# Tail fill, edge-list load and router width in a graph network kernel

## The chip, the cores and the metric

The program runs on one core of one Trainium2 chip. The metric is the device time of one execution in microseconds. Engines: TensorE (PE; its weight loads are shown as PEld), VectorE (DVE), ScalarE (ACT), GpSimd (POOL) and SyncE (SP). SP, ACT and POOL issue DMAs, each on a queue of its own.

## The reference, cut to what matters

Two layers over 6,250 nodes of 256 features and 100,000 edges sorted by destination. Layer 0: a graph step (sum of `x[src]` by `dst`, two products with batch norm between) beside linear attention over all nodes, then a mixture of 32 experts in which each node goes to one. Layer 1: two weighted graph convolutions beside a second attention, then slice attention.

```python
x = x + gnn0(xn, src, dst, edge_weight, ...) + attention0(xn)
# the mixture that the change touches, xf = layernorm(x)
logits = xf @ router_w.T + router_b          # 32 columns
idx = argmax(logits, axis=-1)
h   = relu(einsum('nd,ndh->nh', xf, W1[idx]) + b1[idx])   # 256 -> 64
out = relu(einsum('nh,nhd->nd', h, W2[idx]) + b2[idx])    # 64 -> 256
x = x + out
x = x + gcn1(layernorm(x), src, dst, edge_weight) + attention1(layernorm(x))
x = x + slice_attention(layernorm(x))
```

## The kernel before, in words

The kernel is a row of stages. Inside a stage each engine has its own program, and semaphores order them. A stage ends in a barrier of all engines, after which POOL clears the stage's semaphores and a second barrier follows, so time saved inside one stage moves all that follows forward. Most stages walk over 25 units of up to 256 nodes (49 tiles of 128) through `pipeline`, which interleaves an engine's steps at fixed lags in program order.

1. `stage_setup` (lines 231 to 403). POOL fills constants; SP loads the edge lists (lines 259 to 262: `src`, `dst`, `edge_weight`, each as 97 rows of 1,024 edges and one row of 672), waits for all six loads, then loads 18 weights and bias vectors (line 254) and writes `d_dst` (line 281). DVE waits for the six loads at line 335, casts and checks, and PE and DVE then turn the four lists in 32 rounds over two PSUM banks: one transpose of 98 x 128 (line 389), one copy of 128 x 98 (line 353). Then the weights are turned (lines 399 and 403).
2. `stage_front` (line 406): layer norm, keys and values of the first attention.
3. `stage_aggregate` three times (one for layer 0, two for layer 1): POOL gathers 784 tiles of 128 source rows by indirect DMA (line 1222), DVE builds a selection matrix, PE multiplies (line 1293). Not touched.
4. `stage_gnn_first` and `stage_gnn_second`: batch norm and products.
5. `stage_route` (lines 1736 to 1945). Per unit: ACT ReLU (1812), PE turns back (1908), DVE adds (1841) and takes moments, POOL the root (216), DVE normalises into `accT` (222), PE turns (118), ACT copies to `xnT` (1818), PE multiplies by the router `rT` of 32 columns (1921), DVE adds the bias (1847) and picks the expert; per two units PE counts ranks (1933 to 1937), DVE makes the slots (1871 to 1876), and POOL scatters four tiles of rows into `d_xs` (1803), where each expert owns a region of 50 pages of 128 rows. After the last unit DVE writes `tail_row`, the first free row of each region (1880), and the tables of which expert and page each of 80 tiles has (1881 to 1899).
6. `stage_experts` (line 1948). 80 tiles. For tile t POOL reads the page number from `tile_page` and loads 128 rows (`xt`, 1997), SP loads two weights of the tile's expert (2010, 2011), PE turns the tile (2023), DVE copies (2056), PE multiplies (2032), ACT ReLU (2084), PE multiplies (2040), ACT ReLU (2090) and ACT sends `y` (2094). Buffers are four deep. Behind the last row of each region 128 rows have to be zero. These fills, one DMA of 128 x 256 zeros per expert (1982), are made here: ACT fills the even experts, POOL the odd ones, one ahead. Before POOL loads tile t < 32 it waits for the fill of expert t. ACT issues the fill of expert t+2 after it has seen that of t landed, and in its program order after the `send` of tile t-2; POOL issues the fill of t+2 ahead of the load of t. After tile 31 there are no fills.
7. `stage_second_front`, the second and third aggregation, `stage_heads`, `stage_out`.

The wait that ties loads to fills, and the order in which ACT takes its steps:

```python
if t % 2 == 1 and t + 2 < EXPERTS:
    fill(pool, t + 2, filled_pool)
if t < EXPERTS:
    pool.wait_ge((filled_pool if t % 2 else filled_act)[t // 2 % 2], 16 * (t // 4 + 1))
...
tiles(act, (refill, 0), (relu_h, 0), (relu_y, 1), (send, 1))
```

Of the kernel before, what the change touches and what calls it, by code (L numbers as in the profile page):

```python
# [230 lines left out]
def stage_setup(nc, kit, a, d):  # L231

    k = kit
    with Stage(nc, kit) as st:
# [13 lines left out]
        nload = [0]  # L248

        with nc.Block() as block:  # L250
            @block.sync
            def _(sp):
                def load(dst, src):
                    sp.dma_start(dst, src, allow_slow_non_contiguous=True).then_inc(wld, 16)
                    nload[0] += 1
                full, rest = E // GE, E % GE
                sp.wait_ge(mset, 1)
                for n, name in enumerate(("src", "dst")):
                    sp.dma_start(epad_i[0:full, n, :], a[name][0:full * GE].rearrange("(g e) -> g e", e=GE)).then_inc(eld, 16)
                    sp.dma_start(epad_i[full:full + 1, n, 0:rest], a[name][full * GE:E].rearrange("(g e) -> g e", g=1)).then_inc(eld, 16)  # L260
                sp.dma_start(eew[0:full, :], a["edge_weight"][0:full * GE].rearrange("(g e) -> g e", e=GE)).then_inc(eld, 16)
                sp.dma_start(eew[full:full + 1, 0:rest], a["edge_weight"][full * GE:E].rearrange("(g e) -> g e", g=1)).then_inc(eld, 16)
                sp.wait_ge(eld, 96)
# [17 lines left out]
                sp.dma_start(d.dst.rearrange("(g e) -> g e", e=GE), epad_i[0:NG, 1, :]).then_inc(eld, 16)  # L281
                sp.wait_ge(eld, 112)
                sp.wait_ge(wld, 16 * nload[0])
# [40 lines left out]
            def _(dve):  # L324
# [9 lines left out]
                dve.wait_ge(eld, 96)  # L334
# [15 lines left out]
                for out, _ in dst:  # L350
                    for u in range(GT):
                        dve.wait_ge(tdone, kk + 1)
                        dve.tensor_copy(out.rearrange("p (g u) -> p g u", u=GT)[:, :, u], k.bank[kk % 2][:, 0:NG]).then_inc(cdone, 1)
                        kk += 1
# [20 lines left out]
            def _(pe):  # L375
# [10 lines left out]
                for x in (esrc, edst, rel, eew):  # L386
                    for u in range(GT):
                        b = go()
                        pe.transpose(b[:, 0:NG], x[0:NG, u * P:(u + 1) * P], k.ident[0:NG, 0:NG]).then_inc(tdone, 1)
# [1345 lines left out]

def stage_route(nc, kit, a, d):
# [4 lines left out]
    with Stage(nc, kit) as st:  # L1741
# [4 lines left out]
        tstart = st.sb("tstart", [P, EXPERTS])  # L1746
        with Stage(nc, kit) as sr:
# [10 lines left out]
            count = sr.sb("count", [P, EXPERTS])  # L1758
            ones = sr.sb("ones_h", [P, P], BF16)
# [8 lines left out]
            r_done, back, x1_done, turned, xnT_done, lg_psum, lg_done, ranked, one_done, placed, counted, slot_done, numbered, tab_done, tab_turned = (  # L1768
                sr.sem(n) for n in "r_done back x1_done turned xnT_done lg_psum lg_done ranked one_done placed counted slot_done numbered tab_done tab_turned".split())
            gpool = sr.sem("gpool")  # L1770
            sent = sr.pool_dma("sent")
# [9 lines left out]
            with nc.Block() as block:  # L1781
                @block.sync
                def _(sp):
# [7 lines left out]
                    pipeline(sp, (load, 0), (store, 3))  # L1791
                    x1.all_sent(sp)

                @block.gpsimd
                def _(pool):
# [8 lines left out]
                    pipeline(pool, (lambda u: nm.root(pool, u, gpool), 2), (scatter, 7))  # L1804
                    pool.wait_ge(sent, 16 * NTILE)

                @block.scalar
                def _(act):
# [10 lines left out]
                    pipeline(act, (relu, 0), (copy_xnT, 3))  # L1819

                @block.vector
                def _(dve):
                    n = [0]

                    def then(ins):
                        n[0] += 1
                        ins.then_inc(ranked, 1)
                        dve.wait_ge(ranked, n[0])
                    dve.memset(one[:, LASTT:NTILE, :], 0.0)
# [726 lines left out]
```

## Time and profile before

| what | value |
|---|---|
| runs shown | 4180.55, 4184.23, 4201.93 us (median 4184.23) |
| profiled execution | 4179.45 us, span 4178.0 us |
| busy share | PE 70%, PEld 53%, DVE 44%, ACT 19%, POOL 63% |
| mean granted TensorE clock | 0.858 |
| DMA | 501.67 MB, mean 120 GB/s |

The stages lie at these times of the span, read off their first and last rows: setup 0 to 77.4 us, front to 196.4, first aggregation to 1240, batch-norm stages to 1373.5, routing to 1520.2, experts to 1767, second front to 1898, the other aggregations to 3985, heads and output to 4178.

A page's busy share is a mean over all of these. For a change that touches three stages, the views cut to those stages are the ones to read. In a timeline row the columns are start, duration, engine, line, operation, tiles and count; in brackets is the idle time before it and what ended it. A timeline row with a count above 1 merges neighbours, and its duration is from the first start to the last end. One product in 32-bit floats is two records of PE; a transpose is one.

### The profile page before, as it was taken

What the parts mean: (1) busy time and instruction counts of PE and PEld (TensorE: products, weight loads), DVE (VectorE), ACT (ScalarE), POOL (GpSimd) and SP (SyncE); (2) the same over time, 40 slices, a digit from 0 to 9 for tenths busy, and PEclk for the clock granted to TensorE, in tenths of its full rate; (3) what the DMA queues carried; (4) which work ended last, traced back from release to release, by engine and by line L of the source; (5) the groups of instructions that cost most, each with busy time, mean ns of one, the idle gap of its engine ahead of it and who ended that gap; (6) DMA issues with size and microseconds to landing.
All of it is one profiled execution on the core that took longest, in us unless ns stands there. A gap on an engine that the chain in (4) does not pass through costs nothing. (4 is left out here: it accounts for less than half of the span.)

```text
span 4178.0 us, 41741 instructions
## 1 busy us (share of the span) xinstructions
PE 2928.2 (70%) x13016; PEld 2216.1 (53%) x13016; DVE 1827.8 (44%) x3387; ACT 781.5 (19%) x1777; POOL 2616.7 (63%) x2695
## 2 busy tenths in 40 slices
PE   2867777777768745696776766666577777777768
PEld 2755555555544633584655544444355555555547
DVE  3644444444444730273333333332255555555533
ACT  0411111111113311231111111000022222222220
POOL 1277777777760331256777777777577777777701
PEclk9988888888888556998888888888699999999969
DMA  1334444444432433683444433333344444444405
GB/s 61 99 115 119 120 120 119 120 119 119 118 104 90 138 104 115 193 278 105 119 119 116 120 106 110 106 109 110 92 121 126 126 126 126 127 127 125 124 26 187
DMA packets 280442, 501.67 MB, mean 120 GB/s; under 512 B 61259, under 2 KB 180689, under 8 KB 280074
## 3 DMA queue, kind: packets, MB, share of 16 engines
q0 software_dynamic: 126528, 346.64, 28.9%
q1 hardware_dynamic: 139852, 139.57, 10.7%
q10 hardware_dynamic: 13824, 12.59, 0.9%
q8 instruction: 113, 1.85, 0.2%
q14 instruction: 125, 1.02, 0.1%
HBM read 412.72 MB, written 85.58 MB: 119 GB/s over the span
## 5 line engine op out<-in xcount | busy, mean ns | idle before, releaser
L1293 PE MATMUL bank<-g,m 128*128 128x256 f32 (+1 forms) x4704 | 1568.4, 461 | 923.9 <-DMA g<-d_t,src_i 590.7
L1222 POOL DMA_INDIRECT g<-d_t,src_i x1568 | 1572.5, 1003 | 521.1 <-issue 520.8
L1293 PEld LDWEIGHTS bank<-g,m 128*128 128x128 f32 x4704 | 924.2, 224 | 1253.1 <-issue 574.3
L1222 POOL DMA_INDIRECT g<-d_xn,src_i x784 | 791.9, 1010 | 255.1 <-issue 255.1
L1244 DVE TENSOR_TENSOR eq<-iota,rel_f 128x1024 bf16<-128x1024 f32 x294 | 357.7, 1217 | 457.4 <-PE bank L1293 400.7
L1257 DVE TENSOR_TENSOR accT<-bank,accT 128x256 f32 x294 | 122.7, 417 | 573.2 <-PE bank L1281 572.9
L1247 DVE TENSOR_TENSOR m<-eq,ew_f 128x1024 f32<-128x1024 bf16 x294 | 360.1, 1225 | 10.1
L1228 ACT ACTIVATE s<-bank 128x256 f32<-128x256 f32 (+1 forms) x294 | 111.6, 380 | 1005.6 <-PE bank L1293 551.8
L1997 POOL DMA_DIRECT2D xt<-d_xs x80 | 43.0, 538 | 168.9 <-issue 166.7
L1163 PE MATMUL bank<-wg,side_lg 128*128 128x256 f32 (+1 forms) x392 | 142.7, 457 | 2.9 <-DVE side_lg L1155 2.9
L1295 PE MATMUL bank<-ones_b,eq 128*128 128x1 bf16 x784 | 139.6, 178 | 0.0
L216 POOL TENSOR_TENSOR rsd<-ved,mhalf 128x2 f32<-128x2 f32 (+1 forms) x25 | 18.8, 754 | 188.5 <-DVE ved L210 188.3
L171 POOL DMA_DIRECT2D out<-y x25 | 17.8, 714 | 177.4 <-DVE y L2406 177.4
L2056 DVE COPY xT<-bank 128x256 f32<-128x256 f32 x80 | 34.0, 425 | 200.0 <-PE bank L2023 200.0
L1281 PE MATMUL bank<-ident,s 128*128 128x128 f32 x588 | 119.9, 288 | 0.0
L1255 DVE TENSOR_TENSOR dinv<-bank,dinv 2x128 f32 x98 | 27.4, 279 | 188.8 <-PE bank L1281 188.8
L2023 PE MATMUL bank<-ident,xt 128*128 128x128 f32 x160 | 41.6, 350 | 92.4 <-DMA xt<-d_xs 92.2
L216 POOL TENSOR_TENSOR rsa<-vea,mhalf 128x2 f32<-128x2 f32 (+1 forms) x25 | 17.5, 701 | 141.0 <-DVE vea L210 141.0
L1295 PEld LDWEIGHTS bank<-ones_b,eq 128*128 128x128 bf16 x784 | 87.5, 112 | 34.5
L676 DVE SCALAR_TENSOR_TENSOR side_q<-side_e,side_q 128x256 f32<-128x256 f32 (+1 forms) x49 | 20.9, 427 | 182.7 <-ACT side_q L669 182.7
L1128 PE MATMUL bank<-wxs,m 128*128 128x512 f32 (+1 forms) x196 | 95.6, 611 | 2.7 <-ACT m L1120 2.7
L1281 PEld LDWEIGHTS bank<-ident,s 128*128 128x128 f32 x588 | 84.8, 150 | 23.5 <-issue 3.7
(386 smaller groups left out, 4401.5 us busy)
## 6 DMA issues: line engine op xcount, KB each, us to landing
g<-d_t,src_i POOLq DMA_INDIRECT x1568, 2.8
g<-d_xn,src_i POOLq DMA_INDIRECT x784, 2.8
side_xn<-d_xn SPq DMA_DIRECT2D x96, 128.0 KB, 2.5
d_x<-x SPq DMA_DIRECT2D x48, 256.0 KB, 3.6
d_swT<-wkv SPq DMA_DIRECT2D x48, 256.0 KB, 3.7
swT<-d_swT SPq DMA_DIRECT2D x24, 512.0 KB, 3.4
xt<-d_xs POOLq DMA_DIRECT2D x80, 128.0 KB, 2.6
d_ys<-y ACTq DMA_DIRECT2D x80, 128.0 KB, 2.3
```

The costliest lines, as they stand in the source:

```text
L1128: ins = pe.matmul(k.bank[6][0:w, :], self.xnT3[i % 2][:, c, 0:w], k.wxs[:, c, :], start=(c == 0), stop=(c == C - 1))
L1163: pe.matmul(k.bank[3 + q // 2][:, q % 2 * D:(q % 2 + 1) * D], sw, self.xn3[i % self.LG][0:w, :], start=(i == 0 and q % 2 == 0), stop=last ...
L1222: pool.indirect_dma_start(g[n % RING][:, u, 0:D], None, table, bass.IndirectOffsetOnAxis(ap=k.src_i[:, t:t + 1], axis=0)).then_inc(gathere ...
L1228: act.activation(s[n % 2][:], k.bank[n % 2][:, 0:SW], ACT.Copy).then_inc(copied, 1)
L1244: dve.tensor_tensor(eq[r][:], k.iota[:].rearrange("p (a n) -> p a n", a=1).to_broadcast([P, GT, P]), k.rel_f[:, e].rearrange("p (u a) -> p ...
L1247: dve.tensor_tensor(m[r][:], eq[r][:], k.ew_f[:, e].rearrange("p (u a) -> p u a", a=1).to_broadcast([P, GT, P]), ALU.mult).then_inc(m_done, 1)
L1257: dve.tensor_tensor(at, chunks(k.bank[7]), at, ALU.add).then_inc(acc_added, 1)
L1281: ins = pe.transpose(k.bank[7][:, c * P:(c + 1) * P], s[n % 2][:, c * P:(c + 1) * P], k.ident[:])
L1293: ins = pe.matmul(b[:, 0:GW], m[o][:, u, :], g[r][:, u, :], start=(u == 0), stop=(u == GT - 1 and not count))
L1295: ins = pe.matmul(b[:, GW:SW], eq[o][:, u, :], k.ones_b[:, 0:1], start=False, stop=(u == GT - 1))
L1997: pool.dma_start(xt[r][:], pages[bass.ds(x, 1), :, :].rearrange("a p d -> p (a d)")).then_inc(x_loaded[r], 16)
L2023: ins = pe.transpose(k.bank[j][:, c * P:(c + 1) * P], xt[r][:, c::C], k.ident[:])
```

## The change

- Setup: each list is loaded as 96 rows of 1,024, one row of 1,024 cut into 16 parts, and one row of 672 cut into 16 parts: nine DMAs on SP. The weights are loaded by ACT, which waits for nothing. Four transposes go into one bank, and one copy of 392 columns takes them out: 8 rounds in place of 32.
- Routing: the router is copied into `wide_rT`, whose columns 32 to 127 are zero, so each router product has 128 columns; the bias add reads the first 32.
- Tails: the `zero` tile and the fills move into the routing stage. When `tail_row` is written, SP fills experts 0, 3, ..., 30 (11 fills), ACT 1, 4, ..., 31 (11) and POOL 2, 5, ..., 29 (10, behind its scatters). Semaphores count runs of four fills of one queue, and POOL waits for a tile's run ahead of its load.

```diff
@@ stage_setup
+                for to, name in ((epad_i[:, 0, :], "src"), (epad_i[:, 1, :], "dst"), (eew[:], "edge_weight")):
+                    for g, n, w in ((0, even, GE), (even, full - even, GE), (full, 1, rest)):
+                        sp.dma_start(to[g:g + n, 0:w].rearrange("g (c e) -> g c e", c=(16 if n == 1 else 1)),
+                                     a[name][g * GE:g * GE + n * w].rearrange("(g c e) -> g c e", g=n, c=(16 if n == 1 else 1))).then_inc(eld, 16)
+                sp.wait_ge(eld, EDGE_LOADS)
+                sp.dma_start(d.dst.rearrange("(g e) -> g e", e=GE), epad_i[0:NG, 1, :]).then_inc(eld, 16)
+            @block.scalar
+            def _(act):
                 def load(dst, src):
-                    sp.dma_start(dst, src, allow_slow_non_contiguous=True).then_inc(wld, 16)
+                    act.dma_start(dst, src, allow_slow_non_contiguous=True).then_inc(wld, 16)
...
-                    for u in range(GT):
+                    for u in range(0, GT, 4):
                         b = go()
-                        pe.transpose(b[:, 0:NG], x[0:NG, u * P:(u + 1) * P], k.ident[0:NG, 0:NG]).then_inc(tdone, 1)
+                        for q in range(4):
+                            ins = pe.transpose(b[:, q * NG:(q + 1) * NG], x[0:NG, (u + q) * P:(u + q + 1) * P], k.ident[0:NG, 0:NG])
+                        ins.then_inc(tdone, 1)
@@ new class
+class Tails:
+    QUEUES, RUN = 3, 4
...
+    def fill(self, eng, q):
+        for n, e in enumerate(range(q, EXPERTS, self.QUEUES)):
+            row = eng.value_load(self.k.tail_row[0:1, e:e + 1], min_val=0, max_val=EXPERTS * REGION * P - P)
+            eng.dma_start(self.d.xs[bass.ds(row, P), :], self.zero[:]).then_inc(self.filled[q][n // self.RUN], 16)
+    def landed(self, eng, e):
+        if e < EXPERTS:
+            q, n = e % self.QUEUES, e // self.QUEUES
+            run = n // self.RUN
+            total = len(range(q, EXPERTS, self.QUEUES))
+            eng.wait_ge(self.filled[q][run], 16 * min(self.RUN, total - run * self.RUN))
@@ stage_route
+                    sp.wait_ge(tails_known, 1)
+                    tails.fill(sp, 0)
                     x1.all_sent(sp)
...
                     pipeline(pool, (lambda u: nm.root(pool, u, gpool), 2), (scatter, 7))
+                    pool.wait_ge(tails_known, 1)
+                    tails.fill(pool, 2)
                     pool.wait_ge(sent, 16 * NTILE)
...
-  ins = pe.matmul(k.bank[2 + u.n % 2][0:w, j * EXPERTS:(j + 1) * EXPERTS], xnT[u][:, c, j * P:j * P + w], k.rT[:, c, :], ...)
+  ins = pe.matmul(k.bank[2 + u.n % 2][0:w, j * P:(j + 1) * P], xnT[u][:, c, j * P:j * P + w], wide_rT[:, c, :], ...)
@@ stage_experts
-                    if t % 2 == 1 and t + 2 < EXPERTS:
-                        fill(pool, t + 2, filled_pool)
-                    if t < EXPERTS:
-                        pool.wait_ge((filled_pool if t % 2 else filled_act)[t // 2 % 2], 16 * (t // 4 + 1))
+                    tails.landed(pool, t)
...
-                tiles(act, (refill, 0), (relu_h, 0), (relu_y, 1), (send, 1))
+                tiles(act, (relu_h, 0), (relu_y, 1), (send, 1))
```

## Rows read from the trace of the kernel before

**Rows 1.** Groups of the page: gathers of layer 1 (busy, mean ns, idle before).

```profile
L1222 POOL DMA_INDIRECT g<-d_t,src_i x1568 | 1572.5, 1003 | 521.1 <-issue 520.8
```

**Rows 2.** Waits in the setup (total us, times, longest).

```profile
DVE esrc L335 <- DMA eew<-in_edge_weight: 38.5, 1, 38.5
```

**Rows 3.** Windows of the setup: span; busy by engine; PEclk, DMA share, GB/s.

```profile
23.00:52.00 29.00, 0.00 (x0) 0.00 (x0) 0.00 (x0) 0.00 (x0) 0.00 (x0) 1.00 0.06 26
52.00:62.00 10.00, 2.85 (x10) 1.74 (x10) 7.62 (x20) 0.00 (x0) 0.00 (x0) 1.00 0.64 190
```

**Rows 4.** Timeline of the setup, in order of time.

```profile
3.84 0.35 SPq L259 DMA_DIRECT2D epad_i<-in_src  x1
...
7.79 5.70 DVE L333 CAST iota<-iota_i 128x128 f32<-128x128 int32 x1 [7.79 <-POOL mhalf L318]
7.97 5.44 POOL L320 MEMSET dinv<- 128x6400 f32 x1
...
58.08 0.56 PE L389 MATMUL bank<-ident,esrc 98*128 98x98 f32 x2 [58.08 <-DVE okc L347]
...
71.34 0.56 DVE L353 COPY ew_f<-bank 128x98 f32<-128x98 f32 x2 [0.29 <-PE bank L389]
```

**Rows 5.** Single lines: copies out of PSUM in the setup, ns min/median/max.

```profile
L353 DVE COPY ew_f<-bank x8: 332/334/338, 68.8 to 71.6; 128x98 f32<-128x98 f32 x8
L367 DVE COPY w2T<-bank x2: 424/424/425, 74.8 to 75.3; 128x256 f32<-128x256 f32 x2
```

**Rows 6.** Windows of routing, of tiles 0 to 29 and of tiles 30 to 79.

```profile
1374.00:1499.00 125.00, 94.73 (x492) 85.81 (x492) 98.12 (x361) 38.97 (x75) 59.23 (x67) 0.50 0.46 145
1520.20:1664.70 144.50, 68.22 (x233) 53.64 (x233) 14.66 (x41) 18.00 (x57) 26.04 (x48) 0.59 0.37 113
1664.70:1764.00 99.30, 78.94 (x408) 57.89 (x408) 24.66 (x53) 32.55 (x103) 25.78 (x48) 0.96 0.68 197
```

**Rows 7.** Timeline: four router products; two products of 128 columns.

```profile
1424.67 1.91 PE L1921 MATMUL bank<-rT,xnT 128*128 128x32 f32 x8
...
1529.64 1.06 PE L2032 MATMUL bank<-xT,w 128*128 128x128 f32 x4
```

**Rows 8.** Groups of lines in routing: the router product (busy, mean ns, idle before).

```profile
L1921 PE MATMUL bank<-rT,xnT 128*128 128x32 f32 (+1 forms) x196 | 46.8, 403 | 2.1 <-ACT xnT L1818 2.1
```

**Rows 9.** Waits in routing.

```profile
DVE lgall L1847 <- PE bank L1921: 15.4, 13, 3.2
```

**Rows 10.** The end of routing: timeline, and POOL's drain at the barrier (ns).

```profile
1500.72 0.17 DVE L1880 SCALAR_TENSOR_TENSOR tail_row<-iota,count 1x32 int32<-1x32 f32 x1
...
1507.69 1.57 POOL L1803 DMA_INDIRECT d_xs<-accT,slot  x1 [0.30 <-issue]
...
1520.19 0.27 DVE L2045 MEMSET zero<- 128x256 f32 x1 [15.41 <-PEq L92]
L1781 POOLq DRAIN  x1: 4048/4048/4048, 1513.7 to 1513.7; - x1
```

**Rows 11.** Timeline of the experts: tile 0, tile 30, tile 79.

```profile
1521.85 0.63 POOL L1982 DMA_DIRECT2D d_xs<-zero  x1 [12.59 <-issue]
1524.42 0.57 POOL L1997 DMA_DIRECT2D xt<-d_xs  x1 [1.93 <-issue]
1525.60 0.55 POOL L1982 DMA_DIRECT2D d_xs<-zero  x1 [0.62 <-issue]
1526.95 0.68 PE L2023 MATMUL bank<-ident,xt 128*128 128x128 f32 x2 [22.85 <-DMA xt<-d_xs]
...
1664.70 0.70 PE L2023 MATMUL bank<-ident,xt 128*128 128x128 f32 x2 [5.42 <-DMA xt<-d_xs]
...
1758.76 0.40 PE L2023 MATMUL bank<-ident,xt 128*128 128x128 f32 x2
```

**Rows 12.** Waits in the experts' first 144 us.

```profile
PE bank L2023 <- DMA xt<-d_xs: 92.2, 20, 22.8
```

More of the change, by code:

```diff
@@ L248, in stage_setup @@
         nload = [0]
+        EDGE_LOADS = 16 * 9
         with nc.Block() as block:
@@ L1733, in own_rows, with __init__ @@
     return Kept(lambda u: k.accT[:, :, u.n * BODY:(u.n + 1) * BODY])
+class Tails:
+    QUEUES, RUN = 3, 4
+    def __init__(self, st, k, d, zero):
+        self.k, self.d, self.zero = k, d, zero
+        runs = -(-EXPERTS // (self.QUEUES * self.RUN))
+        self.filled = [[(st.pool_dma if q == 2 else st.sem)(f"filled{q}_{r}") for r in range(runs)] for q in range(self.QUEUES)]
+    def fill(self, eng, q):
[8 more added lines that the diff above has]
+            eng.wait_ge(self.filled[q][run], 16 * min(self.RUN, total - run * self.RUN))
 def stage_route(nc, kit, a, d):
@@ L1767, in stage_route @@
             nm = PipedNorm(sr, "d", x1, xn=own_rows(k))
-            r_done, back, x1_done, turned, xnT_done, lg_psum, lg_done, ranked, one_done, placed, counted, slot_done, numbered, tab_done, tab_turned = (
-                sr.sem(n) for n in "r_done back x1_done turned xnT_done lg_psum lg_done ranked one_done placed counted slot_done numbered tab_done tab_turned".split())
+            r_done, back, x1_done, turned, xnT_done, lg_psum, lg_done, ranked, one_done, placed, counted, slot_done, numbered, tab_done, tab_turned, widened = (
+                sr.sem(n) for n in "r_done back x1_done turned xnT_done lg_psum lg_done ranked one_done placed counted slot_done numbered tab_done tab_turned widened".split())
             gpool = sr.sem("gpool")
+            tails_known = sr.sem("tails_known")
             sent = sr.pool_dma("sent")
@@ L1819, in _ @@
                     pipeline(act, (relu, 0), (copy_xnT, 3))
+                    act.wait_ge(tails_known, 1)
+                    tails.fill(act, 1)
                 @block.vector
@@ L1828, in then @@
                         dve.wait_ge(ranked, n[0])
+                    dve.memset(wide_rT[:, :, EXPERTS:P], 0.0).then_inc(widened, 1)
+                    dve.tensor_copy(wide_rT[:, :, 0:EXPERTS], k.rT[:]).then_inc(widened, 1)
+                    then(dve.memset(zero[:], 0.0))
                     dve.memset(one[:, LASTT:NTILE, :], 0.0)
@@ L1879, in _ @@
                     dve.wait_ge(counted, BATCHES)
-                    dve.scalar_tensor_tensor(out=k.tail_row[:], in0=k.iota[0:1, 0:EXPERTS], scalar=float(REGION * P), in1=count[0:1, :], op0=ALU.mult, op1=ALU.add)
+                    dve.scalar_tensor_tensor(out=k.tail_row[:], in0=k.iota[0:1, 0:EXPERTS], scalar=float(REGION * P), in1=count[0:1, :], op0=ALU.mult, op1=ALU.add).then_inc(tails_known, 1)
                     then(dve.tensor_scalar(pages_i[:], count[:], float(P - 1), None, ALU.add))
@@ L1967, in stage_experts @@
         sent = [st.sem(f"y_sent{j}") for j in range(DEEP)]
[L1968 to L1969 removed]
+        mine_done, start_done = st.sem("mine_done"), st.sem("start_done")
         padded, turned, xT_done, hid, h_done, out_psum, y_done = (st.sem(n) for n in "padded turned xT_done hid h_done out_psum y_done".split())
@@ L1978, in tiles @@
                         step(p - lag)
-        def fill(eng, e, done):
-            r = eng.value_load(k.tail_row[0:1, e:e + 1], min_val=0, max_val=EXPERTS * REGION * P - P)
-            eng.dma_start(d.xs[bass.ds(r, P), :], zero[:]).then_inc(done[e // 2 % 2], 16)
         with nc.Block() as block:
@@ L2044, in _ @@
             def _(dve):
-                dve.memset(zero[:], 0.0).then_inc(blank, 1)
                 for j in range(DEEP):
@@ L2071, in _ @@
             def _(act):
-                act.wait_ge(blank, 1)
-                fill(act, 0, filled_act)
-                def refill(t):
-                    if t % 2 == 0 and t + 2 < EXPERTS:
-                        act.wait_ge(filled_act[t // 2 % 2], 16 * (t // 4 + 1))
-                        fill(act, t + 2, filled_act)
                 def relu_h(t):
```

39 lines of the change are left out of this document (16 added, 23 removed).

## The prediction

> **What bounds the kernel now.** The page's busy shares are read first and put aside: PE is at 70%, POOL at 63%, and no engine is full. Three quarters of the span are three aggregations paced by POOL's gathers, 1,568 in layer 1 [rows 1] and half as many in layer 0, and the change touches none of them. What it touches lies in three stages separated by barriers, so each stage's own last wait is the one to read.
>
> Setup: waits, then windows, then the timeline. DVE waits 38.5 us for the last edge list [rows 2]. In that time DMA moves 26 GB/s at a share of 0.06, which is one engine of 16 (1/16 = 0.0625); the loads after it move 190 GB/s at 0.64 [rows 3]. Then 32 rounds of turn and copy run from 58.08 to 71.34 + 0.56 = 71.90 [rows 4].
>
> Experts: the first PE row of a tile shows its place. Tiles 30 to 79 come at a pitch of (1758.76 - 1664.70)/49 = 1.92 us; tiles 0 to 30 take 1664.70 - 1526.95 = 137.75 us, 4.59 us each [rows 11]. In the slow part PE waits 92.2 us for `xt` [rows 12] and is half idle (68.2 busy in 144.5 us; 78.9 in 99.3 in the other part [rows 6]). The difference in code is the fill: `xt` waits for a fill, and ACT issues the next one only after earlier tiles have gone through.
>
> Routing: DVE is the busiest with 98.1 of 125 us, and PE has 94.7 at half clock, 1.2 GHz [rows 6]. DVE waits 15.4 us in all for the router product [rows 9].
>
> **The change, part by part.**
>
> *Edge lists.* What is late once the lists come fast is DVE itself: its cast of `iota` takes 5.70 us beside POOL's memset of `dinv` and ends at 7.79 + 5.70 = 13.49 [rows 4]. The lists are 1.2 MB and held one engine for 1.2/0.026, about 46 us, so 46/16 = 2.9 us of all 16. The weights and `d_dst` take 0.64 x 10 = 6.4 us of all 16 [rows 3]. Were both queued at 3.84 [rows 4], all would be moved by 3.84 + 9.3 = 13.1 and, with some 2 us to land, known at 15. But ACT starts its weights earlier, since it waits for nothing, and only the lists matter to DVE: at best nine issues at about 0.5 us end at 8.3, and the lists land by 11. I take 13.49, with 0 to +2 us; there is no gain beyond, as the cast is untouched. DVE starts on the lists at 13.49 where it started at 52.0 (13.49 + 38.5): **-38.5 us**. The weights are wanted only after the rounds.
>
> The trace shows no load of 96 rows. The Trainium skill, "DMA: Bandwidth & Descriptors", section "Why a DMA increments its semaphore by 16 and not by 1", says that a transfer is split over the largest number of engines up to 16 that divides the slowest dimension of both sides. That makes 97 rows one engine, as the row of 26 GB/s shows, and 96 rows sixteen. By that rule the term is -38.5; were it wrong for this shape, the term would be 0, which is rival D.
>
> *Rounds.* A turn is one record of 128 columns. Four such records take 1.06 us at half clock [rows 7], of which the last one's 0.40 [rows 8] is latency, so (1.06 - 0.40)/3 = 0.22 us from start to start, 0.88 a round of four. The copy of 392 columns is not shown: it lies between 0.42, the copy of 256, and 4 x 0.334 = 1.34 [rows 5]. From 98 to 256 columns the slope is 0.57 ns, which would give 0.50, but this copy writes with a stride; I take 0.65, nearest the longer copy's row. With two banks PE sets the round: 8 x 0.88, plus 0.2 for the last turn's latency and 0.65 for the last copy, 7.9 us. Before: 71.90 - 58.08 = 13.8. **-5.9 us**; with copies of 1.34 it is 8 x 1.34 + 1 = 11.7, so -2; with turns of 98 columns cheaper in proportion, -7.
>
> *Router.* Four products (8 records) of 32 columns take 1.91 us, two of 128 columns (4 records) 1.06, both at half clock [rows 7]. Start to start that is (1.91 - 0.40)/7 = 0.216 and (1.06 - 0.40)/3 = 0.22: the narrow record already comes as slowly as the wide one, so padding costs PE's stream nothing, and at most 0.05 us a unit at the end, 1 us. The copy and two memsets at the stage's head (0.6 us of DVE) lie in DVE's wait for the first rows; uncovered they cost that. I take **0**; the bounds are +2 and -12 (rival B).
>
> *Fills, at the end of routing.* SP and ACT have nothing left but waits when `tail_row` is there at 1500.89 [rows 10]. Their 11 fills each, at about 1 us an issue (register load, checks, DMA), end by 1513; behind SP's stand only the waits for `x1`. POOL's 10 fills are queued behind its scatters, which end at 1509.26 [rows 10]. One POOL DMA with its register load takes 1525.60 - 1524.42 = 1.18 us [rows 11], so they end at 1521.1. Before, POOL had seen its last scatter land at 1513.7 and drained for 4.05 us, 0.083 for each of its 49 scatters [rows 10]; that it goes by the count is an estimate, and 59 then make 4.9. So POOL ends 7.4 + 0.8 = **8.2 us** later (7.4 if the drain is fixed). Do the transfers hold it? 32 fills are 4.19 MB; at 197/0.68 = 290 GB/s with all engines [rows 6] that is 14.5 us from 1501, and 3 for the last seven scatters: 1519. If the achieved 197 GB/s is the limit, 21 + 5: 1527. Covered by POOL's issues, or +6.
>
> *Experts.* The first load no longer waits for a fill. POOL's first DMA comes 1521.85 - 1520.19 = 1.66 us after the stage's start [rows 10, 11], and it is now `xt`; so tile 0 is turned 1524.42 - 1521.85 = 2.6 us earlier in the stage. With the shift of 8.2 that is 1526.95 + 8.2 - 2.6 = 1532.6; the first weights land about 1 us behind it, inside the spread. From there 30 tiles at 1.92 reach tile 30 at 1590.2 where it was 1664.7: **-74.5 us**, routing's 8.2 included. What is late next is what sets tiles 30 to 79: POOL needs 1.18 of 1.92 us, DMA is at 0.68, PE busy 0.79 [rows 6]. Bounds of the pitch: 1.6, about PE's busy time per tile there (78.9/50), and 2.45 (rival C).
>
> *Sum.* -38.5 - 5.9 + 0 - 74.5 = -118.9. Span 4178.0 - 118.9 = 4059.1; the profiled execution lies 1.45 us over its span, so **4060.6 us**. That execution (4179.45) is 4.8 us below the median of the runs shown; taken from the median it would be 4065. I say 4061.
>
> **The rivals.**
>
> *A, the forecast.* 4061, own range 4047 to 4075 (landing +2, rounds +4, transfers +6, pitch 1.92 +- 0.2 over 30 tiles +-6, the execution's place +5).
>
> *B, the wide router raises the clock in routing.* For it: routing stays at 0.50 with PE busy 76% of the time, while the slow expert tiles, busy 47% with products of 128 and 256 columns, get 0.59 [rows 6]; with 128 columns routing looks more like those. Against: they too were mostly at half clock. Price: PE's times halve and DVE loses most of its 15.4 us of waits [rows 9], but it stays the bound at 98 of 125 us; about -12. 4049.
>
> *C, the early tiles stay at half clock.* For it: the stage starts after some 20 us with hardly any PE work. Against: after 1664.7 the same work reached a mean of 0.96 [rows 6]. At 1.2 GHz a tile is 2 turns and 4 records of 128 columns (6 x 0.22) and 2 records of twice the columns (0.86 by proportion): 2.2 us of PE, and with the hiccups that lift 1.6 to 1.92 near 2.45; over 30 tiles +16. 4077.
>
> *D, the lists do not come faster.* If 96 rows still ran on one engine, the 38.5 us stay and only rounds and experts gain: 4061 + 38.5 = 4099. For it only that no row shows the shape.
>
> *E, slower than before.* The aggregations' gathers slow down, their indices coming from the new copies and POOL's queue having other DMAs before them. There are 2,352, so 118.9/2352 = 51 ns more for each eats the whole gain, and beyond that the kernel is slower; at 60 ns more it is 4061 + 141 = 4202. For it: POOL's issues have no slack in those stages (1,572.5 busy and 521 of issue gaps [rows 1]), so any nanosecond counts in full. Against: nothing in these stages changes, and indices and tables are the same.
>
> **How the numbers follow.** A 0.60, B 0.18, C 0.14, D 0.05, E 0.03. The time is A's. The range reaches down over most of B and up over C: 4042 to 4084, which leaves out D, E and the ends of B and A, under 2 in 10. About 0.5%, 21 us, is what a measurement tells from no change; A to D lie beyond it. Faster 0.96, same 0.01, slower 0.03.
>
> **What would show it.** Setup: DVE's first cast of a list at 13.5, the DMA share before it far over 0.06, the next stage 44 us earlier. Routing: PEclk 0.50 (A) or higher (B), its length up to `tail_row` unchanged; POOL's last fill about 20 us after `tail_row`, the barrier 8 us later than now. Experts: PE's wait for `xt` nearly gone, 80 tiles at 1.92, tile 79 about 152 us after tile 0 where it was 232. Aggregations: gathers at 1,003 ns. The prediction is wrong if the early tiles wait for something else at more than 2.4 us each, or if the fills' transfers and not POOL's issues end the routing by far more than 6 us.

## The result, and the profile after

The changed kernel takes 4068.97 us (median of 4, 4066.72 to 4070.11); the kernel before, run beside it, 4182.66 us (4180.55 to 4201.93). The ratio is 0.9708 [0.9686, 0.973]. The profiled execution took 4068.98 us with a span of 4067.2. Forecast were 4061 us and a range of 4042 to 4084.

Each stage ends in a barrier. Read at the barriers, to 0.1 us, the 110.8 us of span come from here:

| stretch | before | after | difference | forecast |
|---|---|---|---|---|
| setup | 76.5 | 35.0 | -41.5 | -44.4 |
| up to the start of routing | 1297.0 | 1296.4 | -0.6 | 0 |
| routing | 144.5 | 146.4 | +1.9 | +8.2 |
| experts | 248.1 | 168.0 | -80.1 | -82.7 |
| second front | 133.4 | 135.1 | +1.7 | 0 |
| aggregations of layer 1 | 2132.2 | 2139.9 | +7.7 | 0 |
| rest | 146.3 | 146.4 | +0.1 | 0 |

The aggregations of layer 1 end at a barrier at 4031.7 us before, not at 3985: POOL's queue is through there (its last gather ends at 3978.0), but PE, DVE and ACT work on the last tiles for some 47 us more.

**Setup.** The timeline of the changed kernel, answering to [rows 4]:

```profile
7.79 5.70 DVE L337 CAST iota<-iota_i 128x128 f32<-128x128 int32 x1 [7.79 <-POOL mhalf L322]
...
16.09 0.69 DVE L339 CAST esrc<-epad_i 98x1024 f32<-98x1024 int32 x1 [2.60 <-DMA eew<-in_edge_weight]
...
22.17 1.54 PE L394 MATMUL bank<-ident,esrc 98*128 98x98 f32 x8 [22.17 <-DVE okc L351]
...
28.77 1.60 DVE L357 COPY ew_f<-bank 128x392 f32<-128x392 f32 x2 [0.27 <-PE bank L394]
```

DVE's wait of 38.5 us [rows 2] has become one of 2.6 us, and it starts on the lists at 16.09 where it did at 52.0. The rounds run from 22.17 to 28.77 + 1.60 = 30.37, 8.2 us where they were 13.8; a copy of 392 columns takes 0.80 us.

The windows: the loads of the setup (answering to [rows 3]), routing and the experts from tile 0 to the barrier (to [rows 6]), and two of 4 us at the end of routing. Columns are span, busy time of PE, PEld, DVE, ACT and POOL, PEclk, DMA share, GB/s.

```profile
0.00:14.00 14.00, 0.00 (x0) 0.00 (x0) 5.70 (x1) 0.00 (x0) 11.38 (x24) 1.00 0.82 215
1332.00:1452.00 120.00, 78.34 (x488) 68.59 (x488) 97.63 (x360) 38.97 (x75) 58.62 (x66) 0.74 0.49 151
1484.10:1645.80 161.70, 125.14 (x640) 87.29 (x640) 37.50 (x83) 50.64 (x160) 41.76 (x78) 0.98 0.67 195
1468.00:1472.00 4.00, 0.00 (x0) 0.00 (x0) 0.00 (x0) 0.00 (x0) 1.08 (x2) 0.50 1.02 334
1472.00:1476.00 4.00, 0.00 (x0) 0.00 (x0) 0.00 (x0) 0.00 (x0) 0.00 (x0) 0.50 0.53 177
```

Where 26 GB/s on one engine were, the DMA share is now 0.82; the weights, which ACT loads at the same time, are in it. In routing the granted clock is 0.74 and no longer 0.50, and PE is busy 78 us in 120. The experts have a mean of 0.98, where the first 30 tiles had 0.59; only their first 6 us are at half clock (below).

**Routing.** DVE's wait for the router product is 12.2 us (15.4 in [rows 9]):

```profile
DVE lgall L1889 <- PE bank L1963: 12.2, 11, 3.4
```

The end of routing on the timeline, and the drain of POOL's queue at the barrier (ns), answering to [rows 10]:

```profile
1454.89 0.17 DVE L1922 SCALAR_TENSOR_TENSOR tail_row<-iota,count 1x32 int32<-1x32 f32 x1
...
1455.81 14.17 ACTq L1754 DMA_DIRECT2D d_xs<-zero  x10
...
1456.06 13.91 SPq L1754 DMA_DIRECT2D d_xs<-zero  x10
...
1461.86 1.58 POOL L1838 DMA_INDIRECT d_xs<-accT,slot  x1 [0.30 <-issue]
1463.44 4.39 POOL L1754 DMA_DIRECT2D d_xs<-zero  x8
1468.37 0.55 POOL L1754 DMA_DIRECT2D d_xs<-zero  x1 [0.54 <-issue]
1470.23 0.54 POOL L1754 DMA_DIRECT2D d_xs<-zero  x1 [1.32 <-issue]
L1814 POOLq DRAIN  x1: 7178/7178/7178, 1470.4 to 1470.4; - x1
```

`tail_row` is written 1454.89 - 1331.4 = 123.5 us into the stage (127.2 before), so 3.7 us earlier. From the end of the last scatter to the barrier it is now 14.3 us (8.7 before), so 5.6 us more. -3.7 + 5.6 is the +1.9 of the stage. Eight of POOL's ten fills go back to back at 0.55 us.

**Experts.** Timeline of tile 0, then the turn of all 80 tiles as one line (ns min/median/max, first and last start), answering to [rows 11]:

```profile
1481.59 0.55 POOL L2028 DMA_DIRECT2D xt<-d_xs  x1 [10.82 <-issue]
...
1484.11 0.67 PE L2054 MATMUL bank<-ident,xt 128*128 128x128 f32 x2 [25.84 <-DMA xt<-d_xs]
L2054 PE MATMUL bank<-ident,xt x160: 277/281/489, 1484.1 to 1638.3; 128*128 128x128 f32 x160
```

Tile 79 comes 154.1 us after tile 0, a mean pitch of 1.95 us. The first tiles are no slower, though PE had been idle for 25.8 us before them and the clock is still at half in them. The window of the first 5.9 us, and the turn of tile 4, the first at full clock:

```profile
1484.10:1490.00 5.90, 5.47 (x19) 4.09 (x20) 1.57 (x4) 0.99 (x3) 2.53 (x5) 0.53 0.66 180
1490.67 0.40 PE L2054 MATMUL bank<-ident,xt 128*128 128x128 f32 x2
```

Tiles 0 to 3 take (1490.67 - 1484.11)/4 = 1.64 us each; their rows and weights had been loaded ahead. PE's waits there, answering to [rows 12], and those of SP's queue, which loads the weights:

```profile
PE bank L2054 <- DMA xt<-d_xs: 26.2, 2, 25.8
```

```profile
SPq L2040 <- PE bank L2071: 3.2, 8, 0.6
```

Of the 26.2 us, 25.8 lie before tile 0 and are the barrier; the wait for `xt` among the tiles is gone.

**Aggregations.** The gathers of layer 1, answering to [rows 1]:

```profile
L1228 POOL DMA_INDIRECT g<-d_t,src_i x1568 | 1582.2, 1009 | 519.1 <-issue 519.1
```

9.7 us more busy and 2.0 less idle: the +7.7 of the table is the gathers' own time, 6 ns each. Those of layer 0, 784 of the same kind, are not slower (1010 ns before, 1009 after).

### The profile page after: what moved, and what is told of

Same layout as the page of the kernel before. It is cut to its first block and busy times, and to the rows that moved or that the text cites. A ratio compares the mean times of both kernels' runs of the same rounds, so it can differ in the third digit from the quotient of the medians.

```text
span 4067.2 us, 41741 instructions
## 1 busy us (share of the span) xinstructions
PE 2875.3 (71%) x13016; PEld 2167.7 (53%) x13016; DVE 1826.0 (45%) x3365; ACT 781.6 (19%) x1777; POOL 2622.7 (64%) x2689
## 5 line engine op out<-in xcount | busy, mean ns | idle before, releaser
L1299 PE MATMUL bank<-g,m 128*128 128x256 f32 (+1 forms) x4704 | 1545.5, 455 | 941.3 <-DMA g<-d_t,src_i 618.7
L1228 POOL DMA_INDIRECT g<-d_t,src_i x1568 | 1582.2, 1009 | 519.1 <-issue 519.1
L1299 PEld LDWEIGHTS bank<-g,m 128*128 128x128 f32 x4704 | 910.2, 220 | 1264.0 <-issue 607.6
L1228 POOL DMA_INDIRECT g<-d_xn,src_i x784 | 791.4, 1009 | 256.0 <-issue 256.0
L171 POOL DMA_DIRECT2D out<-y x25 | 17.8, 714 | 177.4 <-DVE y L2428 177.4
L682 DVE SCALAR_TENSOR_TENSOR side_q<-side_e,side_q 128x256 f32<-128x256 f32 (+1 forms) x49 | 20.8, 425 | 173.9 <-ACT side_q L675 173.9
L1185 ACT ACTIVATE wkv<-bank 128x512 f32<-128x512 f32 (+1 forms) x49 | 29.2, 596 | 354.7 <-PE bank L1178 354.7
L1170 PEld LDWEIGHTS bank<-ones,side_lg 128*128 128x128 f32 (+1 forms) x392 | 85.8, 219 | 15.6
L2439 PE MATMUL bank<-wkv,swT 128*128 128x256 f32 (+1 forms) x392 | 87.0, 386 | 6.8 <-DMA swT<-d_swT 6.8
```

The costliest lines, as they stand in the source:

```text
L1170: ins = pe.matmul(k.bank[5][:, q:q + 1], sw, k.ones[0:w, 0:1], start=(i == 0 and q == 0), stop=last and q == HEADS * SLICES // P - 1)
L1228: pool.indirect_dma_start(g[n % RING][:, u, 0:D], None, table, bass.IndirectOffsetOnAxis(ap=k.src_i[:, t:t + 1], axis=0)).then_inc(gathere ...
L1299: ins = pe.matmul(b[:, 0:GW], m[o][:, u, :], g[r][:, u, :], start=(u == 0), stop=(u == GT - 1 and not count))
L2439: ins = pe.matmul(k.bank[4 + u.n % 4][0:w, j * D:(j + 1) * D], swT[u][:, j, c * P:c * P + w], k.mout[:, c, :], start=(c == 0), stop=(c == ...
```

## The experiments

The first four ran together (the kernel before took 4198.63 us there). The next four ran on one other chip and the three after them on a second, where every kernel took some 9% longer, the one before too (4556.5 and 4593.33), nearly all of it in the aggregations; ratios and stages are compared, not times across them. The last ran beside a kernel before of 4192.19. Where the main stages came out (us; the last two columns are the aggregations of layer 1 and the mean of its gathers in ns):

| kernel | setup | routing | experts | aggregations | gather |
|---|---|---|---|---|---|
| before | 76.5 | 144.5 | 248.1 | 2132.2 | 1003 |
| after | 35.0 | 146.4 | 168.0 | 2139.9 | 1009 |
| e1 setup alone | 35.1 | 143.8 | 252.6 | 2128.4 | 999 |
| e2 fills alone | 76.3 | 148.9 | 167.8 | 2137.4 | 1005 |
| e3 router alone | 76.2 | 139.5 | 250.7 | 2134.3 | 1005 |
| e4 weights behind | 32.4 | 145.0 | 167.7 | 2151.0 | 1013 |
| e5 97 rows | 75.2 | 145.6 | 170.5 | 2395.1 | 1022 |
| e6 one queue | 34.9 | 158.4 | 168.0 | 2380.8 | 1022 |
| e7 two queues | 35.4 | 146.8 | 165.8 | 2381.4 | 1028 |
| e8 fills ahead | 76.4 | 144.1 | 173.9 | 2376.9 | 1024 |
| e9 weights by ACT too | 32.4 | 145.5 | 177.4 | 2408.3 | 1028 |
| e10 as e9, 6 fills on POOL | 32.4 | 145.5 | 179.2 | 2409.9 | 1022 |
| e11 after, again | 34.6 | 145.4 | 169.0 | 2415.0 | 1027 |
| e12 weights by POOL too | 32.4 | 146.2 | 186.3 | 2144.7 | 1009 |

### e1: the setup alone

The kernel before with the diff's edits in the setup and no others, in their core:

```diff
-  sp.dma_start(epad_i[0:full, n, :], a[name][0:full * GE]...)
+  for g, n, w in ((0, even, GE), (even, full - even, GE), (full, 1, rest)): sp.dma_start(...)
-  for u in range(GT):
+  for u in range(0, GT, 4):
```

> The kernel before with the setup's part of the change alone: lists in 96 rows, weights on ACT's queue, four turns to a bank. In the changed kernel's trace the stage after the setup starts at 35.87 us where it was 77.40. If the parts add up, this run is 41.5 us faster than before and nothing else moves. A rival reading of the changed kernel: its second and third aggregations were 7.3 us longer in all than those of before (gathers of 1,009 ns against 1,003). If the new copies of the indices cause that, this run shows it too and gains only 34 us; if it is the spread from one execution to another, the gathers here lie anywhere between 1,003 and 1,009 ns with no tie to the change.

Measured: 4145.63 us, ratio 0.987 [0.9842, 0.9898]. Setup ends at 35.1, routing is as before, and its window shows the clock of before:

```profile
1337.00:1457.00 120.00, 93.39 (x480) 84.72 (x480) 94.71 (x342) 38.54 (x75) 57.99 (x65) 0.50 0.47 150
```

By its stage the setup gives its 41 us by itself. The whole time fell by 53 us, more than the 41.5 expected; so did e2's (87 us for 76 by its stages), so part of both lies in how the kernel before ran beside them, and the stages are what is compared here. The new copies that write the indices do not slow the gathers: at 999 ns these are the fastest of all. That was one of rival E's two reasons; the other, other DMAs in POOL's queue before the gathers, is tried in e2 (1005 ns against 1003). (The experts, untouched, take 252.6 and in e3 250.7 us where before had 248.1: their early tiles scatter by that much.)

### e2: the fills alone

The kernel before with `Tails` and the fills at the end of routing; router product and setup untouched:

```diff
+  sp.wait_ge(tails_known, 1); tails.fill(sp, 0)      # the same for ACT (1) and POOL (2)
-  fill(act, 0, filled_act)                           # and every fill among the tiles
```

> The kernel before with the fills moved alone: three queues at the end of routing, no fills among the experts; the router keeps its 32 columns and the setup is the old one. By the changed kernel's trace the 80 tiles come at 1.95 us each and routing ends 5.7 us later after its last scatter: tile 79 about 73 us earlier than before, and the whole about 73 us faster. Routing's clock stays at 0.50. If early tiles at full clock in the changed kernel needed the wider router ahead of them, this run's first tiles are slower and the gain is nearer 60. If moved fills disturb the later gathers, the second and third aggregations are some 7 us longer, and those of the run with the setup's part alone are not.

Measured: 4111.61 us, ratio 0.9791 [0.9763, 0.9818]. Routing is 4.4 us longer, the experts 80.3 shorter. The windows are routing, tiles 0 to 79, and the first 6 us of them:

```profile
1374.60:1500.30 125.70, 94.87 (x492) 85.88 (x492) 99.79 (x373) 38.68 (x75) 60.62 (x68) 0.50 0.46 147
1528.50:1683.00 154.50, 121.72 (x624) 88.87 (x625) 36.86 (x82) 48.13 (x153) 41.86 (x78) 0.96 0.69 200
1528.50:1534.50 6.00, 5.39 (x19) 4.02 (x20) 1.52 (x4) 0.99 (x3) 2.64 (x5) 0.50 0.62 180
```

A routing stage at half clock is followed here by four tiles at half clock and all others at full clock, as in the changed kernel. So it does not take the wide router to bring the clock up; rival C's half clock holds for four tiles of its 30 and costs nothing that shows, and the 76 us of routing and experts together (316.7 where they were 392.6) belong to the fills alone.

### e3: the wide router alone

```diff
-  b[0:w, j*EXPERTS:(j+1)*EXPERTS], xnT[u][:, c, ...], k.rT[:, c, :]
+  b[0:w, j*P:(j+1)*P], xnT[u][:, c, ...], wide_rT[:, c, :]
```

> The kernel before with the router padded to 128 columns alone. If the padding is what raised routing's granted clock from 0.50 to 0.73, this run shows about 0.73 in routing too, the table of free rows is written 3.7 us earlier after the stage's start, and the kernel is about 4 us faster (within what rounds can tell). If the clock rose for another reason, such as the different time at which the stage starts, routing stays at 0.50 and the kernel is the same within 1 us. The experts should be unchanged at 4.59 us a tile up to tile 30.

Measured: 4190.61 us over 10 executions, ratio 0.9986 [0.9972, 1.0001]. In time that is not told from no change. In the profile routing is 4.9 us shorter, and its window, and one group of eight records of the router's product at half clock, are:

```profile
1377.60:1503.00 125.40, 75.14 (x494) 65.68 (x494) 102.57 (x387) 38.98 (x75) 63.21 (x70) 0.79 0.48 149
1406.87 2.08 PE L1925 MATMUL bank<-wide_rT,xnT 128*128 128x128 f32 x8
```

The same products on PE, four times as wide in the router, and the granted clock goes from 0.50 to 0.79; PE is busy 75 us instead of 95. That is rival B's mechanism. It holds in every profile: the ten with the wide router show 0.73 to 0.80 over 120 us of routing and `tail_row` 122.1 to 123.9 us into the stage, the four with the narrow one (before, e1, e2, e8) 0.50 and 126.6 to 127.2. At half clock the eight wide records take 2.08 us where the narrow ones took 1.91 [rows 7]. The stage gains little, because DVE was and stays its bound (102.6 of 125.4).

### e4: the weights behind the lists

```diff
 def _(act):
+    act.wait_ge(eld, EDGE_LOADS)
     load(raw["L0_gnn_w1"][:], ...)
```

> The changed kernel with ACT waiting for all nine list loads before it issues the weights. In the changed kernel DVE took up the lists at 16.09 us, 2.6 us after its cast had ended. If the weights' transfers beside them held the lists back, the lists land before 13.49 here, DVE takes them at 13.5, and the setup is 2.6 us shorter; the weights are issued from about 11 to 20 us and land before PE asks for them at about 29. If the lists are late by their own transfers, DVE starts at 16 as before and nothing is gained; if the weights then come too late, PE waits for them and the setup is longer than 35.9 us.

Measured: 4070.41 us, ratio 0.9685 [0.9654, 0.9717]. Setup ends at 32.4, 2.6 us before the changed kernel's. The timeline of DVE:

```profile
7.80 5.70 DVE L338 CAST iota<-iota_i 128x128 f32<-128x128 int32 x1 [7.80 <-POOL mhalf L323]
13.54 0.69 DVE L340 CAST esrc<-epad_i 98x1024 f32<-98x1024 int32 x1
```

The lists are there when the cast of `iota` ends, as the forecast had it for the changed kernel. ACT, which waits for them, issues its first weight at 11.05: "the lists land by 11" comes true once the lists are alone. The window of 4 to 13 us, in which the changed kernel has a share of 0.97:

```profile
4.00:13.00 9.00, 0.00 (x0) 0.00 (x0) 5.20 (x1) 0.00 (x0) 7.97 (x17) 1.00 0.64 160
```

The 2.6 us that the change was short of are the weights' transfers beside the lists'.

### e5: lists as 97 rows, otherwise the change

```diff
-  for g, n, w in ((0, even, GE), (even, full - even, GE), (full, 1, rest)):
+  for g, n, w in ((0, full, GE), (full, 1, rest)):
```

> The changed kernel with one thing put back: each list is again loaded as 97 rows of 1,024 (the last row of 672 stays cut into 16 parts, the weights stay with ACT). If the row count decides how many engines carry a load, DMA's share falls to about one engine's 0.06 once the weights are through, and DVE takes the lists up at about 50 us in place of 16; the kernel is about 34 us slower than the changed one. If the gain came from splitting the last row or from moving the weights to another queue, DVE still starts at about 16.

Measured: one execution, 4488.59 us. DVE waits for the lists, and in that wait one engine moves:

```profile
56.31 0.69 DVE L338 CAST esrc<-epad_i 98x1024 f32<-98x1024 int32 x1 [42.84 <-DMA eew<-in_edge_weight]
```

```profile
14.00:50.00 36.00, 0.00 (x0) 0.00 (x0) 0.00 (x0) 0.00 (x0) 0.00 (x0) 1.00 0.07 26
```

All of the lists' gain hangs on 96 rows against 97. No changed kernel ran beside this one, so the cost is read off the setup: 75.2 us, where e6 and e7 on the same chip have 34.9 and 35.4. Taking the weights off SP's queue gives nothing: DVE starts at 56.3, later than the 50 expected and than the 52.0 of the kernel before, probably since the weights now move beside the lists. The trace agrees with the Trainium skill's rule on how many engines a transfer gets ("DMA: Bandwidth & Descriptors", "Why a DMA increments its semaphore by 16 and not by 1"): 0.07 at 26 GB/s with 97 rows, 0.64 at 160 with 96 and one apart and no weights beside them (e4).

### e6 and e7: the fills by one queue, by two

```diff
-    QUEUES, RUN = 3, 4
+    QUEUES, RUN = 1, 4      # e6: ACT's alone; e7: 2, SP's and ACT's
```

> The changed kernel with all 32 fills at the end of routing on ACT's queue. An issue without load takes ACT about 0.9 us (register load 0.28, checks 0.2, DMA 0.35), so 32 take 28 us: from 1456 to 1484 us in place of 1472, and the barrier comes at about 1484, some 6 us later than with three queues (1477.7), as POOL's own part is shorter. If the transfers were the limit in the changed kernel (4.19 MB at 284 GB/s, 15 us), one queue would issue no slower than the engines move and the barrier would stay within 2 us of 1477.7.

> The changed kernel with 16 fills each on SP and ACT and none on POOL. If POOL's ten fills and its longer drain set the end of routing in the changed kernel, POOL now ends 17 us after the table of free rows is written, as in the kernel before, at 1472; SP and ACT, at 1.45 us an issue in the changed kernel, need 16 x 1.45 = 23 us to 1479 if that pace is their own, or 15 us if it was the shared transfers. So the barrier lies between 1472 and 1479; nearer 1479 the three queues are worth having only for their issue time.

Measured, one execution each: 4444.71 and 4434.02 us. From `tail_row` to the barrier it is 36.1 us with one queue and 24.8 with two, beside 22.9 with three (23.2 in e5, on the same chip as these two). The fills of e6 and of e7 on the timelines:

```profile
1577.26 34.81 ACTq L1754 DMA_DIRECT2D d_xs<-zero  x32
```

```profile
1580.46 21.18 ACTq L1754 DMA_DIRECT2D d_xs<-zero  x16
1580.72 23.09 SPq L1754 DMA_DIRECT2D d_xs<-zero  x16
```

One queue issues a fill each 1.09 us and ends the stage, 13 us later than three do, more than twice what was expected; two issue one each 0.73 us between them (1.3 and 1.4 for each queue), and the third queue takes off only 2 us more. The Trainium skill ("DMA: Bandwidth & Descriptors", "Issuing engines are not separate DMA queues") says that more issuing engines save only the time of the issue, usually small beside the transfer. The traces agree that it is the issue that is saved; it was not small: 11.3 us from the second queue.

In both, POOL has its 49 scatters and no fill, as in the kernel before. Its drain at the barrier in e7, with the DMA share at 0.67 in those 4 us (the one in e6, at 0.38, is as long):

```profile
L1814 POOLq DRAIN  x1: 4048/4048/4048, 1592.6 to 1592.6; - x1
```

### e8: the fills left among the experts' tiles, but further ahead

```diff
-  if t % 2 == 1 and t + 2 < EXPERTS: fill(pool, t + 2, filled_pool)
+  if t % 2 == 1 and t + 6 < EXPERTS: fill(pool, t + 6, filled_pool)   # ACT: t + 8
```

with three fills ahead at the start on POOL, four on ACT, and four semaphores each in place of two; all else as before.

> The kernel before with the fills left among the experts, but each queue up to four fills ahead in place of one: ACT makes 0, 2, 4, 6 first and then t+8, POOL 1, 3, 5 and then t+6. Nothing is moved to routing, and nothing else is changed. If the 4.59 us of the early tiles were the wait for one fill issued too late, and not the fills' transfers or issues themselves, the early tiles run near 2.0 to 2.3 us (POOL has two DMAs for each odd tile, 1.8 us a tile) and the kernel is about 70 us faster. If the fills' work itself cost the time, it stays near 4.6 and the kernel is the same as before; then only moving them could help.

Measured: 4478.79 us, ratio 0.9821 [0.9778, 0.9865]. The turns of the 80 tiles:

```profile
L2024 PE MATMUL bank<-ident,xt x160: 277/282/487, 1652.6 to 1808.8; 128*128 128x128 f32 x160
```

156.2/79 = 1.98 us a tile, and routing and experts together are 318.0 us (before 392.6, e2 316.7). The same 32 fills among the same tiles cost next to nothing once they are issued early enough. So the 74 us of the early tiles were a wait for a fill issued too late, as the prediction read the code, and neither the fills' bytes nor their issues. Nearly all of the gain could be had without moving the fills to another stage.

### e9, e10 and e11: half of the weights by ACT

After e4, SP had no slack among the experts (3.2 us of waits in 156), so it was the suspect for the pitch of 1.95. In e9 ACT loads `expert_out` for the odd tiles:

```diff
+  if t % 2 == 1: act.dma_start(w2[t % DEEP][0:HID + 1, :], a["expert_out"]...)
```

e10 also gives SP and ACT 13 fills each and POOL 6; e11 is the changed kernel again, beside them.

> The changed kernel with weights behind the lists, and among the experts the second weight of every odd tile loaded by ACT in place of SP. In the changed kernel's trace SP waits for nothing among the experts (3.2 us in all) and issues a tile's two loads every 1.9 us, which is the tiles' pitch of 1.95; PE's own time for a tile is 1.57. If SP's issues set the pitch, taking one DMA of two tiles away (0.46 us) brings the pitch to about 1.7 and 80 tiles gain some 18 us, with the setup's 2.6 us about 20 us over the changed kernel. If the DMA transfers (share 0.67) or the wait of DVE and ACT in turn set it, the pitch stays at 1.95, and only the 2.6 us are gained.

> As the last, with the fills dealt out as 13 on SP, 13 on ACT and 6 on POOL. In the changed kernel POOL ends 22.9 us after the table of free rows is written, SP and ACT end their 11 fills 17 us after it. If POOL's fills and its drain set the end, POOL ends about 3 us earlier here (4 fills at 0.55 us and 0.083 us of drain each) and SP's and ACT's 13 issues at 1.45 us end at 19.9 us: the barrier comes about 20 us after the table. If the transfers set the end (with 16 fills on each of two queues it was 24.8), nothing is gained.

> The changed kernel once more, beside the two others on one chip. Its gain over the kernel before should be 2.7 to 2.9% again. Its gathers' mean duration in the second and third aggregations tells whether the 7.3 us that these stages were longer belong to the kernel: if they do, its layer-1 gathers are again 6 ns slower than those of kernels without the moved fills; if not, they fall anywhere in the spread of 999 to 1,013 ns that four other kernels showed.

Measured: 4480.15 us, ratio 0.9751 [0.9726, 0.9776]; 4481.91, 0.9765 [0.9734, 0.9797]; 4471.3, 0.9726 [0.9698, 0.9754]. A miss. In e9 SP now waits, and PE's weight load waits twice as long for ACT's product `hT` (34.3 us in the changed kernel; the engine's waits over the stage, and those of SP's queue):

```profile
PEld bank L2073 <- ACT hT L2116: 69.9, 80, 1.4
```

```profile
SPq L2041 <- PE bank L2073: 42.8, 69, 1.0
```

```profile
1700.48 0.40 PE L2056 MATMUL bank<-ident,xt 128*128 128x128 f32 x2
...
1702.08 0.40 PE L2056 MATMUL bank<-ident,xt 128*128 128x128 f32 x2
...
1704.64 0.40 PE L2056 MATMUL bank<-ident,xt 128*128 128x128 f32 x2
```

The timeline shows tiles by turns 1.60 and 2.56 us apart: where ACT issues nothing the tile comes at the 1.60 of the prediction's lower bound, and the load on ACT costs more in the other: the register load and the DMA hold ACT from 1701.70 to 1703.15, and the ReLU that makes `hT` starts at 1703.24. The mean is 2.06. e10's split of the fills gives nothing: 23.3 us from `tail_row` to the barrier, as in e9, with SP's thirteenth fill now the last (issued at 1606.6, barrier 1607.4), where it had been POOL's drain.

### e12: half of the weights by POOL

As e4, and the odd tiles' `expert_out` is issued by POOL behind its load of `xt`:

```diff
+  wait(pool, out_psum, t - DEEP + 1)
+  pool.dma_start(w2[t % DEEP][0:HID + 1, :], a["expert_out"]...)
```

> The changed kernel with weights behind the lists, and among the experts the second weight of every odd tile loaded by POOL, which has room: 1.16 us of each 1.95 us tile, 1.7 with this. On ACT the same load sat between its ReLUs: odd tiles took 2.56 us and even ones 1.60. If SP's issues (two DMAs and a register load, 1.9 us a tile) set the changed kernel's pitch of 1.95 to 1.97, it falls to about 1.7 here, SP shows waits, and the experts' stage is some 18 us shorter than 168 us, with the setup's 2.6 us a ratio to the kernel before near 0.967. If the pitch stays at 1.95, something else sets it: the transfers at a share of 0.67, or the turns that PE, DVE and ACT take.

Measured: 4091.87 us, ratio 0.9763 [0.974, 0.9787]. Another miss: tiles at 170.0/79 = 2.15 us, experts 186.3. The waits of the stage:

```profile
PE bank L2064 <- DMA xt<-d_xs: 65.8, 45, 25.2
```

About 40 of these 65.8 us are behind tile 0: POOL's `xt` comes late. Two `xt` and one weight load take POOL 3.84 us where they stand back to back (1562.87 to 1566.71), so 1.92 a tile and not 1.7; and nine weight loads waited for PE, 17.5 us in all, with the next `xt` behind them in the same queue. How the 2.15 divides between the two is not shown. SP, ACT and POOL each hold the pitch at 1.95 or above once they carry this load. That SP alone sets the 1.95 is suggested by the tiles of 1.60 us in e9, not shown: no version with the load on a free queue exists here. None of these versions beats the changed kernel; e4's ratio overlaps both of its own.

## Why the prediction was right

**Setup, -44.4 forecast, -41.5 measured.** The step of the lists holds (e1, e5): one engine of 16 for 97 rows, sixteen for 96, and the cast of `iota` late next. Its size was -38.5 and came out as 16.09 - 52.0 = -35.9. The missing 2.6 us are what e4 gives back: "the lists land by 11" left out that the weights share the engines with them. The rounds were -5.9 and came out as -5.6; the copy took 0.80 us where 0.65 was taken, and PE and DVE wait for each other by turns.

**Router, 0 forecast, -3.7 measured.** Rival B's mechanism, given 0.18, is what happened: the clock rises to 0.74 (0.79 in e3), and only with the wide router. The forecast's step that failed is "for PE's stream it costs nothing, so 0": the stream's cost was nearly right (0.17 us a group of eight at half clock, where 0.05 was allowed), its effect on the granted clock was missed. Only the price of B was too high: -12 was nearly all of DVE's wait for the product, and that wait fell from 15.4 to 12.2 us (10.6 in e3), about what the stage gained. Probably the rest of it is not PE's pace but the chain through ACT's `xnT` before the product; DVE is the stage's bound in either case.

**Fills, +8.2 forecast, +5.6 measured** (from `tail_row` to the barrier 22.87 us where it was 17.23; 22.1 in e2). Two terms erred against each other. POOL's fills were priced at 1.18 us, issue to issue, from a pair of the experts' stage, 11.8 for ten; eight of them took 0.55, since POOL's queue had read their registers while its scatters ran, and the ten ended 1470.77 - 1463.44 = 7.3 us after the last scatter. The drain was put at 4.9 us for 59 DMAs and took 7.18. It begins at 1470.4 while transfers go on at the full DMA share up to 1472 and at 0.53 up to 1476. Transfers of other queues do not lengthen it (e6 and e7: 4.05 us for 49 scatters, as before). Those of POOL's own fills probably do: they take 4.5 us (median) from issue to landing, and in the seven profiles with 59 DMAs the drain is 5.94 to 7.18 us, 1.1 to 2.3 over what the count gives.

```profile
d_xs<-zero POOLq DMA_DIRECT2D x10, 128.0 KB, 4.5
```

The forecast had transfers that hold the end as a bound, +6.

**Experts, -82.7 forecast, -80.1 measured.** Tile 0 stands 1484.1 - 1477.8 = 6.3 us into the stage where it stood 8.95: the 2.6 of the forecast. The pitch is 1.95 and not 1.92, times 79 the other 2.5 us. The reason is shown twice, by removing the fills (e2) and by issuing them earlier (e8). Rival C is excluded by the 0.96 of e2; its 2.45 us for a tile at half clock did not show either, as the four tiles that ran at it came at 1.64. Of the 92.2 us that PE waited for `xt` before [rows 12], 22.8 lay ahead of tile 0 and were never the fills'.

**Aggregations, 0 forecast, +7.7 measured.** This is the largest part of the 8 us by which the forecast was low. No part of the change alone shows it: with the setup alone gathers take 999 ns, with the fills or the router alone 1005. The three executions of the combined kernel and its variants beside a kernel before of usual time show 1009, 1013 and 1009. But in the comparison where all ran longer, e8, which has the setup and router of before, shows 1024 beside 1022, 1022 and 1028 for versions of the changed kernel. Most likely it is the spread between executions; with one profile for each it stays open, and at 6 ns rival E (51 ns) is far off.

**The sum.** 2.9 (setup) - 6.3 (routing) + 2.6 (experts) + 8.9 (the rest) = 8.1 us above the forecast span of 4059.1. The two large terms hold by their mechanism. That the sum is this close is in part luck: routing's two errors, -3.7 for the router and -2.6 for the fills, cancel the +5.5 of setup and experts.

## What to carry to other kernels

A wait in a loop is worth its whole length when what it waits for could have been issued a few turns earlier: look at how far ahead each queue runs before counting bytes, and compare the pitch of the disturbed turns with that of undisturbed ones in the same stage. Look for a DMA share of 1/16 in any window, and cut the shape of such a transfer to a multiple of 16 rows and a remainder. A load moved to a "free" queue puts its own issue (1.45 us on ACT in e9), and any wait for a buffer (e12), before everything that this engine does next; in two trials of two that cost more than the busy queue did.

## What the runs showed of the hardware

- Padding the router's product from 32 to 128 columns lengthened a group of eight records at half clock from 1.91 to 2.08 us and raised the granted clock of the stage from 0.50 to 0.79 (e3), so the stage's PE work fell from 95 to 75 us.
- POOL's drain at a barrier goes by the count of its DMAs where these have landed: 4.05 us for 49 in routing, 7.91 for 96 at the end of the experts before, 6.59 for 80 after, 9.86 for 120 in e12, 0.082 us each. With fills of its own under way it was 5.94 to 7.18 for 59. The rule does not carry on to many: after the 784 gathers of an aggregation the drain ends 6.6 us after the last of them.
- A register load takes longer while several queues' fills are under way. In the fills of the changed kernel, ns min/median/max:

```profile
L1753 ACTq TENSOR_LOAD <-tail_row x11: 291/547/2212, 1455.1 to 1470.0; - x11
L1753 POOLq TENSOR_LOAD <-tail_row x10: 295/542/1456, 1455.1 to 1468.3; - x10
```

  Among the experts before, the median of such a load was 284 ns on ACT, and with one queue (e6) 282. One queue alone never took over 699 ns (e6), two took up to 1643 (e7, medians 274 and 402): part of what a queue needs more for a fill when there are several.
- The same programs took 9% longer on two of the chips used, 2377 to 2415 us for layer 1's aggregations where others show 2128 to 2151, with gathers only 2% slower (1022 to 1028 ns) and 712 to 743 us of idle time between them where it is 519 to 522.
